# A two-layer graph kernel: one quarter of the last products ahead of t's turning, loads and norms reordered, statistics by bn_stats

## The reference

```python
u = par_u[0]*par_u[1]*(diag_u[:, None]*x[:2048] @ W_u) + x[:2048]
i = par_i[0]*par_i[1]*(diag_i[:, None]*x[2048:] @ W_i) + x[2048:]
e = concat(u, i)
h = adj @ (adj.T @ e)                     # t = adj.T @ e
y = layernorm(x + layernorm(h)*gamma + beta + x)
z = dinv[:, None] * (y @ W1)              # dinv = rsqrt(adj.sum(axis=0) + 1)
o = relu(dinv[:, None] * (adj.T @ z + z) + b1)
out = layernorm(y + o)
```

## Time and profile before

| | us |
|---|---|
| median of 3 runs | 641.5 (639.92 to 642.29) |
| the profiled execution | 641.78 |
| its span, first to last instruction | 640.1 |
| PE busy | 600.1 (94%) |
| DVE, ACT, POOL busy | 334.5, 138.8, 108.4 |
| read from HBM | 202.82 MB, mean 320 GB/s |

### The profile page before, as it was taken

How to read it: one execution, slowest core, us unless ns; L and a number is a source line. 1 busy time by engine, 2 the same in 40 slices (tenths; PEclk the granted TensorE clock), 3 DMA queues, 4 the chain that set the end, 5 groups by cost and what they waited for, 6 DMA issues and landing times.

```text
span 640.1 us, 10729 instructions
## 1 busy us (share of the span) xinstructions
PE 600.1 (94%) x4785; PEld 235.2 (37%) x4785; DVE 334.5 (52%) x355; ACT 138.8 (22%) x208; POOL 108.4 (17%) x126
## 2 busy tenths in 40 slices
PE   6989999999999999999999999999999999978775
PEld 5433333333333333333333335554343434313112
DVE  3789467768767776876675782644140402103004
ACT  2015060421506042150605117311000101001001
POOL 3006051240705122050503104100000000000000
PEclk9989999999999999999999999999999999999998
DMA  7998299959778694977879497699999999999991
GB/s 256 387 377 291 98 363 377 388 189 351 269 268 298 240 387 163 372 266 259 290 256 387 150 387 266 244 349 338 383 409 410 410 411 409 412 409 410 412 396 63
DMA packets 86002, 204.82 MB, mean 320 GB/s; under 512 B 4539, under 2 KB 7099, under 8 KB 85957
## 3 DMA queue, kind: packets, MB, share of 16 engines
q1 hardware_dynamic: 84196, 202.77, 85.1%
q10 hardware_dynamic: 1760, 1.38, 0.6%
HBM read 202.82 MB, written 1.31 MB: 319 GB/s over the span
## 4 chain that ended last, share of the span: by engine, by line
PE 76%; DMA 14%; DVE 7%; POOL 1%; ACT 1%; issue 1%; SPq 0%; ACTq 0%; DVEq 0%; POOLq 0%
PE psum L751 28%; PE psum L861 21%; PE psum L954 12%; DMA slot<-in_adj_dram 9%; PE psum L869 6%; DMA last_slot<-in_adj_dram 4%; DVE slot L583 3%; PE psum L795 2%; PE psum L745 2%; PE psum L974 1%; POOL turned L354 1%; DVE turn L562 1%; PE psum L722 1%; PE psum L934 1%; PE psum L922 1%; DVE last_slot L583 1%
## 5 line engine op out<-in xcount | busy, mean ns | idle before, releaser
L583 DVE STREAM_TRANSPOSE slot<-slot 128x2048 f32<-128x2048 f32 x80 | 177.7, 2279 | 75.9 <-PE psum L751 75.9
L751 PE MATMUL psum<-slot,E 128*64 128x512 f32 x768 | 173.8, 603 | 3.0 <-DVE slot L589 2.6
L861 PE MATMUL psum<-slot,T 32*64 32x512 f32 x2560 | 142.5, 590 | 0.0
L354 POOL COPY turned<-last_slot 32x1024 f32<-32x1024 f32 x80 | 84.4, 1055 | 285.8 <-DVE last_slot L583 281.5
L954 PE MATMUL psum<-slot,E 128*64 128x512 f32 x512 | 115.0, 596 | 10.5 <-DMA slot<-in_adj_dram 9.7
L751 PEld LDWEIGHTS psum<-slot,E 128*64 128x64 f32 x768 | 53.2, 138 | 114.4 <-issue 113.4
L404 ACT ACTIVATE turned<-last_slot 32x1024 f32<-32x1024 f32 x80 | 84.3, 1054 | 40.6 <-DVE last_slot L583 38.9
L861 PEld LDWEIGHTS psum<-slot,T 32*64 32x64 f32 x2560 | 55.9, 132 | 84.4 <-issue 84.4
L694 DVE TENSOR_TENSOR T<-psum,dinv 128x256 f32<-128x256 f32 x10 | 4.2, 425 | 144.1 <-PE psum L974 143.7
L395 ACT ACTIVATE T<-T 32x256 f32<-32x256 f32 x60 | 24.8, 414 | 224.1 <-DVE T L567 222.9
L954 PEld LDWEIGHTS psum<-slot,E 128*64 128x64 f32 x512 | 35.2, 137 | 86.5 <-issue 60.0
(11 more groups left out here) (110 smaller groups left out, 268.4 us busy)
## 6 DMA issues: line engine op xcount, KB each, us to landing
slot<-in_adj_dram SPq DMA_DIRECT2D x152, 1024.0 KB, 14.3
last_slot<-in_adj_dram SPq DMA_DIRECT2D x30, 1024.0 KB, 7.7
turned<-in_adj_dram SPq DMA_DIRECT2D x10, 1024.0 KB, 15.1
X<-in_x_dram SPq DMA_DIRECT2D x5, 256.0 KB, 5.1
out_dram<-T ACTq DMA_DIRECT2D x10, 128.0 KB, 5.8
T<-in_L_gnn_W_u_dram ACTq DMA_DIRECT2D x2, 16.0 KB, 2.9
T<-in_L_gnn_W_i_dram ACTq DMA_DIRECT2D x2, 16.0 KB, 4.6
beta_b<-in_L_gnn_ln_beta_dram SPq DMA_DIRECT2D x1, 32.0 KB, 11.5
```

The source lines that it names most:

```text
L354: nc.gpsimd.tensor_copy(turned[c * Q32:(c + 1) * Q32, a].rearrange("p h k j r -> p (h k j) r"), last_blocks[a * Q32:(a + 1) * Q32, :, c, : ...
L583: v.transpose(parts, parts).then_inc(chunk_cut, 1)
L751: return mm(acc[half[b % 2], :], E[:, b, :], view[:, b % CB, :], start=(b < 2), stop=(b >= NB - 2))
L861: last = mm(acc[half[h], a, :], T[step % 2][rows_a, jb, (c - a) % 4, :], slot[step % 2][rows_a, h:NF:2, :, cols], start=False, stop=False, ...
```

## The change

Seven edits go together. The loads of `diag` and `par` move from SP's queue to ACT's, with `diag` ahead of the weights and `par` between `W_u` and `W_i`, and PE turns the first two groups of x before it waits for them. The five matmuls that zeroed PSUM banks are gone, since the first products now start their banks. In step 0, DVE transposes six chunks instead of eight ahead of t's copies; the h products of step 0 stand after 4 and 14 of the twenty pairs of t's sums instead of after 10 and 20. In every step, one quarter of `h_last` stands ahead of `turn_t`, and the first `h_group` waits for the spread copies piece by piece, with its inner order changed from column block to distance `d`. In the hand-over the norm of group 0 runs alone first, `FIRST` takes two chunks of stripe 1 early, the last two quarters of `h_last` come later, and SP issues the two `turned` loads behind the sixth reload. `finish` takes mean and variance by four `bn_stats` and four `bn_aggr` and applies them by four `tensor_scalar`. In the tail both last stripes are copied out by ACT before either is finished, and `turn_o(8)` stands one sweep later.

```diff
+ACT_COPIES = [(a, d) for d in range(1, 4) for a in range(4) if (a + d) % 2]
+DVE_COPIES = [(a, d) for d in range(1, 4) for a in range(4) if (a + d) % 2 == 0]
...
-FIRST = [(0, 0), (0, 1), (0, 2), (0, 3), (1, 0), (1, 1), (1, 2), (1, 3), (0, 4), (0, 5), (1, 4), (1, 5),
+FIRST = [(0, 0), (0, 1), (1, 0), (1, 1), (0, 2), (0, 3), (1, 2), (1, 3), (0, 4), (0, 5), (1, 4), (1, 5),
          (0, 6), (0, 7), (1, 6), (1, 7), (0, 8), (1, 8), (0, 9), (1, 9)]
-FIRST_LOADS = [(s, q) for s, q in FIRST if s == 0 or q >= NF]
+FIRST_LOADS = [(0, q) for q in range(NF)] + [(0, 8), (1, 8), (0, 9), (1, 9)]
+LATE = 6
...
             load_x(0)
-            sp.dma_start(diag[0:USERS // CB, :], diag_u.rearrange("(q j) -> q j", j=JW)).then_inc(scales_loaded, 16)
-            sp.dma_start(diag[USERS // CB:NQ, :], diag_i.rearrange("(q j) -> q j", j=JW)).then_inc(scales_loaded, 16)
-            sp.dma_start(par[:, 0:2], par_u.unsqueeze(0).to_broadcast([P, 2])).then_inc(scales_loaded, 16)
-            sp.dma_start(par[:, 2:4], par_i.unsqueeze(0).to_broadcast([P, 2])).then_inc(scales_loaded, 16)
             for g in range(1, NG):
                 load_x(g)
...
-            for s, q in FIRST_LOADS:
+            def load_first(s, q):
                 m = FIRST.index((s, q))
-                if q < NF:
-                    sp.wait_ge(slots_used, NJ - 1)
-                elif q == NF:
-                    sp.wait_ge(moved_act, NJ * len(ACT_MOVES))
-                    sp.wait_ge(moved_pool, NJ * len(POOL_MOVES))
-                else:
-                    sp.wait_ge(h_done, 2)
                 load(place(m)[0], place(m)[1], q, s)
+
+            sp.wait_ge(slots_used, NJ - 1)
+            for q in range(NF):
+                load_first(0, q)
+            sp.wait_ge(moved_act, NJ * len(ACT_MOVES))
+            sp.wait_ge(moved_pool, NJ * len(POOL_MOVES))
+            for s in range(RES):
+                load_first(s, NF)
 
             for k in range(1, NJ // RES):
                 for m in range(RES * NQ):
+                    if k == 1 and m == LATE:
+                        sp.wait_ge(h_done, 2)
+                        for s in range(RES):
+                            load_first(s, NQ - 1)
                     sp.wait_ge(chunk_swept, (k - 1) * RES * NQ + m + 1)
...
+            act.dma_start(diag[0:USERS // CB, :], diag_u.rearrange("(q j) -> q j", j=JW)).then_inc(scales_loaded, 16)
+            act.dma_start(diag[USERS // CB:NQ, :], diag_i.rearrange("(q j) -> q j", j=JW)).then_inc(scales_loaded, 16)
             act.wait_ge(weights_zeroed, 3)
             load_w(0, WM[:, 0, :], W_u)
+            act.dma_start(par[:, 0:2], par_u.unsqueeze(0).to_broadcast([P, 2])).then_inc(scales_loaded, 16)
+            act.dma_start(par[:, 2:4], par_i.unsqueeze(0).to_broadcast([P, 2])).then_inc(scales_loaded, 16)
             load_w(1, WM[:, 2, :], W_i)
...
+            copy_hT(2, 2)
             square_h(1)
-            for g in (2, 3):
-                copy_hT(g)
-                square_h(g)
-            root_h(1)
             copy_yT(0)
             root_y(0)
+            root_h(1)
+            square_h(2)
             copy_yT(1)
             root_y(1)
             root_h(2)
-            copy_hT(4)
-            square_h(4)
+            square_h(3)
             copy_yT(2)
             root_y(2)
             root_h(3)
             copy_yT(3)
+            root_y(3)
+            copy_hT(4)
+            square_h(4)
             root_h(4)
...
-                for q in range(NF):
+                early = NF - 2 if step == 0 else NF
+                for q in range(early):
                     cut_chunk(step * NQ + q)
                 copy_tT(step)
                 copy_t(step, step % 2)
-                for q in range(NF, NQ):
+                for q in range(early, NQ):
                     cut_chunk(step * NQ + q)
                 if step == NJ - 1:
...
             norm_h(0)
-            norm_h(1)
             restore(1)
             make_group(0)
+            norm_h(1)
             restore(2)
             make_group(1)
             norm_h(2)
             restore(3)
+            restore(4)
             make_group(2)
             norm_h(3)
-            restore(4)
+            restore(5)
+            make_group(3)
             norm_h(4)
-            make_group(3)
-            restore(5)
             restore(6)
+            restore(7)
             make_group(4)
-            restore(7)
...
-                 .then_inc(o_centred, 1)
-                dve.wait_ge(o_squared, J + 1)
-                after(4, v.tensor_reduce(rsum[:, 0:JB], sq, AX, ALU.add))
-                v.tensor_scalar(var[:, 0:JB], rsum[:, 0:JB], 1.0 / F, EPS, ALU.mult, ALU.add).then_inc(o_var, 1)
+                for jb in range(JB):
+                    v.bn_stats(stats[:, jb, :], o[:, jb, :]).then_inc(o_stats, 1)
+                dve.wait_ge(o_stats, JB * (J + 1))
+                if J >= 1:
+                    dve.wait_ge(o_root, J)
+                for jb in range(JB):
+                    v.bn_aggr(mean_var[:, jb, :], stats[:, jb, :]).then_inc(o_var, 1)
...
-
+                for jb in range(JB):
+                    v.tensor_scalar(stage[:, jb, :], o[:, jb, :], mean_var[:, jb, 0:1], r[:, jb:jb + 1],
+                                    ALU.subtract, ALU.mult).then_inc(out_ready, 1)
...
             pe.wait_ge(ident_ready, 1)
+            turn_x(0)
+            turn_x(1)
             pe.wait_ge(scales_loaded, 16 * 4)
             for k in range(CB):
                 last = nc.tensor.transpose(scale_turn[:, k, :], diag[:, k::CB], ident[0:NQ, 0:NQ])
             last.then_inc(diagT_done, 1)
-            turn_x(0)
-            turn_x(1)
...
-            for q in range(1, NQ - 1):
+            for q in range(1, NQ):
                 first_sums(q)
-            pe.wait_ge(xT_ready, NG)
-            for i in range(5):
-                last = mm(bank[i], zeros[:, 0:P], zeros, start=True, stop=True)
-            last.then_inc(banks_zeroed, 1)
-            first_sums(NQ - 1)
...
             def h_group(step, jb):
 
-                for c in range(4):
-                    cols = slice(jb * P + c * Q32, jb * P + (c + 1) * Q32)
+                for d in range(4):
+                    if jb == 0 and d > 0:
+                        pe.wait_ge(spread_act, step * len(ACT_COPIES) + 2 * d)
+                        pe.wait_ge(spread_dve, step * len(DVE_COPIES) + 2 * d)
                     for a in range(4):
+                        c = (a + d) % 4
+                        cols = slice(jb * P + c * Q32, jb * P + (c + 1) * Q32)
                         rows_a = slice(a * Q32, (a + 1) * Q32)
                         for h in range(2):
-                            last = mm(acc[half[h], a, :], T[step % 2][rows_a, jb, (c - a) % 4, :],
+                            last = mm(acc[half[h], a, :], T[step % 2][rows_a, jb, d, :],
                                       slot[step % 2][rows_a, h:NF:2, :, cols],
-                                      start=False, stop=False, skip_group_check=True)
+                                      start=step == 0 and jb == 0 and d == 0, stop=False, skip_group_check=True)
                 return last
 
             def h_last(step, jb):
 
                 for h in range(2):
                     last = mm(bank[4][half[h], :], T[step % 2][:, jb, 0, :], turned[:, :, h, :, jb, :],
-                              start=False, stop=False, skip_group_check=True)
+                              start=step == 0 and jb == 0, stop=False, skip_group_check=True)
                 return last
 
             def h_step(step):
 
 
                 final = step == NJ - 1
-                each = JB // T_ROUNDS
-                for n in range(T_ROUNDS):
-                    if step == 0:
-                        t_pairs(step + 1, n * HS // T_ROUNDS, (n + 1) * HS // T_ROUNDS)
-                    if n == 0:
-                        pe.wait_ge(t_ready, step * 2 + 2)
-                        pe.wait_ge(spread_act, (step + 1) * len(ACT_COPIES))
-                        pe.wait_ge(spread_dve, (step + 1) * len(DVE_COPIES))
-                        pe.wait_ge(chunk_cut, step * NQ + NF)
-                    for jb in range(n * each, (n + 1) * each):
-                        last = h_group(step, jb)
-                        if final and jb == 0:
-                            turn_degrees()
-                    if n == T_ROUNDS - 1:
-                        last.then_inc(slots_used if not final else h_done, 1)
-                    if step > 0 and not final:
-                        t_pairs(step + 1, n * HS // T_ROUNDS, (n + 1) * HS // T_ROUNDS)
-                if not final:
-                    turn_t(step + 1)
-                    pe.wait_ge(moved_act, (step + 1) * len(ACT_MOVES))
-                    pe.wait_ge(moved_pool, (step + 1) * len(POOL_MOVES))
-                    for jb in range(JB):
-                        last = h_last(step, jb)
-                    last.then_inc(turned_used, 1)
-
+                if step == 0:
```

(54 more changed lines are left out.)

69 lines of the change are left out of this document (29 added, 40 removed).

## The result

| | before | after |
|---|---|---|
| median of 6 runs, us | 641.03 (639.75 to 642.29) | 635.52 (633.07 to 637.89) |
| ratio | | 0.9911 [0.9887, 0.9934] |
| profiled execution, its span | 641.78, 640.1 | 634.37, 632.7 |

The change makes the kernel 0.9% faster: 5.5 us between the medians, 7.4 between the two profiled spans. The forecast was 635.3, with faster at 0.85. The total is right, in part by luck. Its parts aren't: the start has the wrong sign, and the steps, the hand-over and the tail made up for it.

A forecast was written before the change was run, and what follows sets the result against it. PE's own order and waits bound the first pass, transfers at about 410 GB/s the second. Gains 5.1 + 1.1 + 0.4 - 0.4 = 6.2 us off 640.1 give 633.9, plus 1.4 for the median: 635.3, range 630.2 to 638.6.

The forecast's parts named there:

- The steps: First pass: a quarter of `h_last` fills PE's 0.74 us wait for DVE's copy; 0.64 a step, 5.1 us in eight.
- I charge 0.1: Steps: cost in us put on one more change of shape on PE when `h_last` is split.
- This shorter cover costs nothing: Steps: the next `h_group` begins 2.7 us behind the turning instead of 3.6, harmless as it waits for copies piece by piece.
- The start: Up to step 1: earlier loads, no zeroing and t taken sooner together gain 1.1 us, bounds 0 and 5.7.
- I put it 0.8 us later: Start: issue of `par` as ACT's sixth instead of SP's fifth; PE's chain still 1.3 us earlier net.
- The bound of 0: Start: lower bound of PE's 1.3 us gain, if `par` lands slower beside the chunks or late `W_i` holds up DVE.
- I expect the same 3.3: Step 0: PE's idling of 3.4 us for the eighth transpose again costs 3.3 us through a lower clock.
- clock that stays up: Rival: PE's clock does not fall in step 0, giving 631.4 us; chance 0.2.
- The hand-over: Between the passes: reloads start later but run denser, the twentieth lands 0.4 us sooner; bounds +2 and -3.
- The tail: Two last `finish`: 4.95 us each for 4.3, the first starting 1.35 later; the end 0.4 us later.
- the rival of a slow pace: Hand-over: transfers stay at 2.95 us a load, costing 6.6 us, 641.9 and no change; chance 0.1.
- The order within `h_group`: Rival: tiles at four different column blocks overlap less, so two products exceed 7.05 us; 646.6 at 8%; chance 0.04.

The follow-up runs named there:

- kernel 2: The changed kernel with all four quarters of `h_last` behind `turn_t` again; 644.82 us, ratio 1.007 to the kernel before.
- kernel 7: The kernel before the change with one edit, a quarter of `h_last` ahead of `turn_t`; 639.56 us, ratio 0.9971.
- kernel 9: The kernel before with two edits: the quarter ahead of `turn_t`, and `h_group` ordered by distance with waits piece by piece; 633.1 us, ratio 0.9872.
- kernel 11: The changed kernel, unaltered, profiled once more for the scatter of its start; one execution, 632.94 us.
- kernel 5: The changed kernel, but SP issues the first chunk only when `diag`, `par`, `W_u` and `W_i` have landed; one execution, 636.84 us.
- kernel 1: The changed kernel with the loads of `diag` and `par` back on SP's queue behind x's first group; 633.28 us, ratio 0.99 to the kernel before.
- kernel 4: The changed kernel with the old hand-over: old orders of PE, DVE, ACT and SP there; 636.25 us, ratio 0.9939 to the kernel before.
- kernel 6: The changed kernel with the old `finish` (two reductions, centring, ACT's square, variance, one product), the tail's new order kept; one execution, 636.19 us.
- kernel 8: The changed kernel with `diag` and `par` on SP's queue, six pairs of sums ahead of the first products, `turn_o(8)` one sweep sooner; 630.71 us, ratio 0.9837.

## Why the prediction was right in total and wrong in its parts

**The steps** (forecast -5.1, measured -6.9). The mechanism is right: the wait for DVE's copy is covered, and kernel 2 brings it back with 0.89 us. The term was mis-sized by "I charge 0.1" for one more change of shape on PE: the split costs 0.01 (0.86 + 2.73 for 3.58), and the turning became 0.07 shorter (1.04 for 1.11). The charge had been derived from a difference of 0.09 between two rows, which was no cost of a split. Without it the waits give the bound of 5.9 and the turning 0.6; what gave the other 0.4 us is not told apart. "This shorter cover costs nothing" was right only with its own condition. Kernels 7 and 9 show it: without the waits piece by piece, 0.54 us a step are lost again, nearly two thirds of the gain.

**The start** (forecast -1.1, measured +1.35, and -0.95 in kernel 11). The first h products began at 52.06 instead of 46.2, 5.9 us late. From there to step 1 it took 32.84 us, the 32.9 of the forecast without its 3.3 for the clock. So two steps failed, in opposite directions. "I put it 0.8 us later" for `par` on ACT's queue: it landed 5.6 us later in the profile, and t's last sums began at 27.39 instead of 22.99, 4.4 later where the forecast had 1.3 earlier. In the six profiles where the changed queues ran beside the chunks, it took 6.9 to 9.0 us from issue to landing; in the three with the order before, 4.4 to 4.9, and some 5 on ACT's queue with the chunks held back (kernel 5). The bound of 0 named the cause (slower beside the chunks' traffic) and put nothing on it. Its other cause, a late `W_i`, was harmless: it landed at 15.8 instead of 8.0, and PE's chain has only 0.09 us of waiting between there and t's last sums (0.2 in kernel 11). The Trainium skill (DMA: Bandwidth & Descriptors, Issuing engines are not separate DMA queues) says that another issuer saves issuing time alone. In the runs it saved that (SP's first chunk goes out 1.4 us sooner) and cost more: `par` then had the chunks beside it and landed later.

"I expect the same 3.3" for the clock was the other. It did not fall in step 0 after 3.52 us of idling in the first profile, nor in kernels 1 (3.34) and 11 (2.56); it fell in kernels 2 (3.52), 4 (3.52), 5 (3.42) and 6 (3.13), and in the old order of step 0 at 2.80 (before, kernels 7 and 9). The same gap of 3.52 us ended both ways, so its length does not decide here, and what does stays open. The rival's 0.2 for a clock that stays up was too low: three of seven executions of this order kept it. A fall cost 1.7 us in kernel 2 (8.82 for 7.13), not 3.3. That is not due to the new order: in kernels 7 and 9, where the twenty matmuls of sums stand behind the gap as before, turning and sums took 11.38 us for some 9.8, so a fall cost 1.6 there too, and before it was 13.02. The 3.3 was the price of one execution, in which the clock stayed down until 49.5; in kernel 9 it was up again by 48.5. S over these executions of the changed start is 82.60 and 84.90 with the clock up, 85.34 and 85.69 where it fell (kernels 6 and 4); before and in kernel 9 it was 83.55 and 83.67. The start thus loses about 1 us on the mean and scatters by 3. That the forecast of it is off by only 2.5 is luck: the late `par` and the spared clock each moved it by more. What the scales' queue alone costs is not told apart: kernel 1's S is 1.0 below the mean of the changed kernel's two with the clock up, and the ratios' intervals overlap (0.9866 to 0.9934 and 0.9887 to 0.9934).

Kernels 2 and 11 have `par` at the same time (10.53, 10.50) and t's last sums start 1.3 us apart (26.39, 25.09). PE's rows show where, first kernel 2's, then kernel 11's:

```profile
14.72 1.06 PE L736 MATMUL psum<-ident,X 128*128 128x128 f32 x4
14.36 0.60 PE L736 MATMUL psum<-ident,X 128*128 128x128 f32 x4
```

The same four transposes take 1.06 and 0.60 us, and the products behind them 2.69 and 1.89: kernel 2's PE stayed at the slow pace longer. The granted clock reads 1.00 in both, so at the start of a profile that reading doesn't tell the pace, and why kernel 2 left the slow pace later stays open.

**The hand-over** (forecast -0.4, measured -1.5 in one pair of profiles). Over all kernels the two orders differ by about 0.4 us in m17 - T, while the values of the new order alone lie 1.3 apart, so 1.1 us of the 1.5 are scatter. The forecast's size stands, but is not proven. The mechanism is shown: the transfers ran at 398 GB/s or more from T + 30 and at 409 from T + 40 (forecast 410 from T + 35), with the old order they did not (kernel 4), and the rival of a slow pace falls.

**The tail** (forecast +0.4, measured -0.4). The path was right, DVE without a break through both `finish`; the term "4 x 0.28 for the statistics, 4 x 0.20 for the aggregates" was too dear. The groups of DVE's lines say why (busy time, mean ns of one):

```profile
L722 DVE TENSOR_SCALAR T<-T,mean_var,rstd 128x64 f32<-128x64 f32 x40 | 9.8, 310 | 0.4
L711 DVE BATCH_NORM_STATS2 stats<-T 128x6 f32<-128x64 f32 x40 | 6.1, 214 | 0.3
L716 DVE BATCH_NORM_AGGREGATE mean_var<-stats 128x2 f32<-128x6 f32 x40 | 3.8, 158 | 0.3
```

One `bn_stats` lasts 0.214 us and one `bn_aggr` 0.158, but forty keep DVE busy for 6.1 and 3.8 us, 0.15 and 0.095 each: the next begins before the last ends. I had added 0.03 between two where they overlap by 0.06. The estimates by the fixed cost that the Trainium skill states (VectorE: DVE Perf Modes, The TRN2 errata), 0.22 and 0.16, agree with the durations of `bn_stats` and `bn_aggr` and not with the pace, so 4.6 us was too much as well. The last products, of 64 columns too, last 0.310 and not 0.22.

A second term was wrong the other way, "The first of the two `finish` starts 1.35 later", since "a sweep of 1.9 stands ahead of its turning". It starts 6.15 us behind m17 where it was 3.77, so 2.4 later. The sweep has a load of its own to wait for:

```profile
618.97 1.94 PE L765 MATMUL psum<-turned,E 128*64 128x512 f32 x8 [0.77 <-DMA turned<-in_adj_dram]
```

The two `finish` of 1.0 us less each more than make up for it, and the tail ends 0.8 us ahead of the forecast. Kernel 8 takes the sweep back, and the end comes another 0.8 us sooner (15.66 for 16.44).

**The order within `h_group`** costs nothing: from step 1 on two products take 7.05 us in all kernels (kernel 7 alone has 7.13 for those right behind its wait for ACT), and that rival falls.

So 1.8 more from the steps, 1.1 from the hand-over and 0.8 from the tail are 3.7; 2.45 of it was lost at the start. What is left, 1.2, is the difference between 633.9 and the measured 632.7. The forecast then put the median 1.4 above the span, and it is 2.8 above the profiled one (635.52), because the executions scatter. So the median matches to 0.2 us by one error that hides another.

## What to carry to other kernels

When a stage lies on the critical engine, look for what its next wait needs before you call its cover free: the quarter alone gave a third of its gain, and with the waits of its consumer cut in pieces nearly all. A small load that everything waits for belongs ahead of the bulk on its queue; on another queue it saves an issue of some 0.4 us and has megabytes beside it. And test a bundle's parts alone: here two edits give the whole gain, the new `finish` 0.6 us, the others little or less than nothing, and with three places set otherwise (kernel 8) the ratio is 0.984 for 0.991.

## What the runs showed of the hardware

- A landing that took 4.4 to 4.9 us with the bulk loads 2.6 us behind it took 6.9 to 9.0 with them beside it, though it is 1 KB.
- TensorE's granted clock after the same idle gap of 3.52 us in the same place was 1.00 (its upper level, 2.4 GHz) in one execution and fell to 0.50 (1.2 GHz) in two others. What a fall costs varies too: in the old order it was 3.3 us in one execution and 1.6 in two. A time that rests on it has a spread of its own.
- At 14.7 us of kernel 2 PE took 1.06 us for four transposes that take 0.60 elsewhere, while the granted clock read 1.00 from 4 us on.
- Small independent operations of DVE in a row overlap: `bn_stats` over 64 columns lasts 0.214 us and comes every 0.15, `bn_aggr` 0.158 and 0.095, `tensor_scalar` over 64 columns 0.310 and 0.245.
- Splitting a run of eight matmuls around another operation cost 0.01 us.
